# The power -1/2 of the head norms on GpSimd, with table loads, copies of x and the mean in other places

## The reference, cut to what matters

```
def l2norm(t):
    return t / jnp.maximum(jnp.linalg.norm(t, axis=-1, keepdims=True), 1e-12)
...
q = l2norm(q) * qs
k = l2norm(k) * ksc
q = q * cos * scale + rotate_half(q) * sin * scale
k = k * cos * inv + rotate_half(k) * sin * inv
out = local_attention(q, k, v)
...
mu = x.mean(-1, keepdims=True)
var = ((x - mu) ** 2).mean(-1, keepdims=True)
xn = (x - mu) / jnp.sqrt(var + 1e-05) * g + bln
return a * jax.nn.gelu(gate, approximate=False) @ W2 + b2
```

## Time and profile before

| | us |
|---|---|
| median of 3 runs | 3920.88 (3917.01 to 3927.07) |
| the profiled execution | 3918.71 |
| its span | 3916.9 |
| PE busy | 3581.4 (91%) |
| DVE busy | 3162.1 (81%) |
| ACT busy | 2652.5 (68%) |
| POOL busy | 2432.0 (62%) |

### The profile page before, as it was taken

How to read it: one execution, slowest core, us unless ns; L and a number is a source line. 1 busy time by engine, 2 the same in 40 slices (tenths; PEclk the granted TensorE clock), 3 DMA queues, 4 the chain that set the end, 5 groups by cost and what they waited for, 6 DMA issues and landing times.

```text
span 3916.9 us, 146395 instructions
## 1 busy us (share of the span) xinstructions
PE 3581.4 (91%) x60128; PEld 2226.2 (57%) x60128; DVE 3162.1 (81%) x4377; ACT 2652.5 (68%) x4972; POOL 2432.0 (62%) x2197
## 2 busy tenths in 40 slices
PE   5676776899999999999999999999999999999997
PEld 2222222566666666666666666666666666666664
DVE  4899998888878778888878788778787887888884
ACT  3555554677777777767776777677777777676765
POOL 0355554876666666666666666666666666666661
PEclk9889898999999999999999999999999999999999
DMA  3000000111111111111110111111111111110101
GB/s 76 0 0 0 0 0 0 34 32 31 31 42 41 34 30 31 31 47 38 35 32 26 42 42 36 32 31 31 45 37 33 31 31 47 36 36 27 32 28 37
DMA packets 64418, 120.05 MB, mean 31 GB/s; under 512 B 18196, under 2 KB 35986, under 8 KB 63634
## 3 DMA queue, kind: packets, MB, share of 16 engines
q1 hardware_dynamic: 63762, 110.70, 9.7%
HBM read 20.50 MB, written 2.10 MB: 6 GB/s over the span
## 4 chain that ended last, share of the span: by engine, by line
PE 53%; DVE 15%; issue 9%; ACT 7%; POOL 0%; ACTq 0%; DMA 0%; DVEq 0%; POOLq 0%; SPq 0%
PE ob L1187 10%; PE qk L1129 9%; PE sc L1214 7%; PE trb L1001 6%; PE vob L1195 4%; PE vob L1135 4%; PE sc L1163 4%; DVE arena L888 3%; PE sc L1221 3%; DVE ssq L894 3%; DVE mx L901 3%; PE ob L1001 2%; DVE arena L889 2%; ACT arena L619 2%; DVE xnT L978 1%
## 5 line engine op out<-in xcount | busy, mean ns | idle before, releaser
L507 POOL TENSOR_TENSOR arena<-arena,rnorm 128x512 f32<-128x512 f32 x768 | 793.7, 1054 | 929.3 <-ACT rnorm L626 928.8
L500 POOL TENSOR_TENSOR arena<-arena 128x512 f32<-128x512 f32 x768 | 961.7, 1274 | 84.9 <-DVE arena L889 84.9
L633 ACT ACTIVATE arena<-trb 128x512 f32<-128x512 f32 x768 | 465.7, 606 | 432.4 <-PE trb L1001 432.4
L1129 PE MATMUL qk<-wqkv,xs 128*128 128x512 f32 x1536 | 734.2, 601 | 16.0 <-issue 8.9
L888 DVE TENSOR_TENSOR arena<-qk,tab_q 128x512 f32<-128x512 f32 x384 | 263.7, 687 | 504.6 <-ACT arena L619 499.6
L483 POOL TENSOR_TENSOR arena<-arena 128x512 f32<-128x512 f32 x256 | 299.9, 1180 | 345.4 <-DVE arena L858 329.9
L1001 PE MATMUL trb<-ident,arena 128*128 128x128 f32 x3072 | 483.0, 280 | 10.7 <-ACT arena L633 7.6
L619 ACT ACTIVATE arena<-qk 128x512 f32<-128x512 f32 x768 | 433.5, 592 | 79.4 <-PE qk L1129 65.5
L1129 PEld LDWEIGHTS qk<-wqkv,xs 128*128 128x128 f32 x1536 | 294.5, 193 | 312.0 <-issue 294.8
L894 DVE TENSOR_REDUCE ssq<-arena 128x16 f32<-128x1024 f32 x384 | 464.3, 1209 | 0.0
L514 POOL TENSOR_TENSOR arena<-arena,rinv 128x512 f32<-128x512 f32 x384 | 392.4, 1043 | 65.8 <-DVE rinv L911 65.8
(11 more groups left out here) (139 smaller groups left out, 6020.5 us busy)
## 6 DMA issues: line engine op xcount, KB each, us to landing
arena<-arena SPq DMA_DIRECT2D x192, 384.0 KB, 3.2
arena<-arena SPq DMA_DIRECT2D x192, 64.0 KB, 3.0
wqkv<-in_L_ffn_Wqkv SPq DMA_DIRECT2D x18, 512.0 KB, 4.3
wo<-in_L_ffn_Wo SPq DMA_DIRECT2D x6, 512.0 KB, 4.0
arena<-in_L_attn_x SPq DMA_DIRECT2D x8, 256.0 KB, 2.8
out<-arena SPq DMA_DIRECT2D x8, 256.0 KB, 2.2
w<-in_L_ffn_W SPq DMA_DIRECT2D x6, 341.0 KB, 2.9
arena<-in_sel SPq DMA_DIRECT2D x1, 1024.0 KB, 5.0
```

The costliest lines, as they stand in the source:

```text
L500: nc.gpsimd.tensor_tensor(ts[c * 2 + j][:, heads], tu[:, 0, heads], tu[:, 1, heads], ALU.add).then_inc(summed[0], 1)
L507: nc.gpsimd.tensor_tensor(part, part, rnorm[j][:, 8 * h:8 * h + 8].unsqueeze(2).to_broadcast([P, 8, HEAD]), ALU.mult) \
L633: A((qT, kT)[j][u][:, 4 * h:4 * h + 4, at_col:at_col + P], TRB.rearrange("p (a t) -> p a t", a=4), ACT.Copy) \
L1129: MM(QK[:, 512 * h:512 * h + 512], lhsT=xs[u][:, c * P:(c + 1) * P], rhs=wqkv[:, col:col + 512], start=True, stop=True) \
```

## The change

- The clamp of the sums of squares moves from DVE to POOL, and POOL raises them to -1/2 by a two-input instruction with the operation pow and a tile filled with -0.5. ACT's logarithm and exponential for the head norms go. The factors 2^32 (in the logarithm) and 2^16 (in the rotary tables) go too.
- The number of table loads stays at four for a group of eight slots. The loads for gelu stand at the end of slots 6 and 0, those back to the exponential's set in slots 0 and 2 ahead of the exps.
- `stage_x` and `stage_norm` stand in slot 2 ahead of the table load and the exps (`stage_x` of slot 6 ahead of its exps); `stage_norm` was at the end of slot 1.
- PE does the mean of slot 3 behind the two products up.

```diff
-LN_SCALE = float(2 ** 32)
...
+        power = sb("power", [P, HEADS])
...
-        ssqc_ready = sem("ssqc_ready")
-        ln_done = sem("ln_done")
+        ssq_open = sem("ssq_open")
+        ssqc_ready = sem("ssqc_ready", 2)
...
+            nc.gpsimd.memset(power[:], -0.5)
...
             def scale(U, B, u, c, j):
                 item(pool, summed, U * 2 + 1)
+                item(pool, ssq_done, U)
+                pool.sem_inc(ssq_open[0], 1)
+                nc.gpsimd.tensor_scalar(ssqc[j][:], ssq[j][:], NORM_FLOOR, None, ALU.max).then_inc(ssqc_ready[0], 1)
+                item(pool, ssqc_ready, U)
+                nc.gpsimd.tensor_tensor(rnorm[j][:], ssqc[j][:], power[:], ALU.pow).then_inc(r_done[0], 1)
                 pool.wait_ge(r_done[0], U + 1)
...
-            def norms(U, B, u, c, j):
-                act_e.wait_ge(ssqc_ready[0], U + 1)
-                A(lnv[j][:], ssqc[j][:], ACT.Ln, scale=LN_SCALE).then_inc(ln_done[0], 1)
-                act_e.wait_ge(ln_done[0], U + 1)
-                slot(act_e, scaled, U * 2 + 1)
-                A(rnorm[j][:], lnv[j][:], ACT.Exp, scale=-0.5).then_inc(r_done[0], 1)
...
-                if up0 or up1:
-                    act_e.preload_act_table(ACT.Gelu)
...
-                if up0 or up1:
+                if k % UNITS == 2:
+                    at_ = unit_at(l, k, -2)
+                    if at_:
+                        stage_x(at_[1], at_[2], (k + 2) // UNITS % BATCH, l + (k + 2) // LAYER)
+                    at_ = group_at(l, k - 1, LAG_STAGE)
+                    if at_:
+                        stage_norm(*at_)
+                if group_at(l, k - 1, LAG_UP[0]) or group_at(l, k - 1, LAG_UP[1]):
                     act_e.preload_act_table_set(EXP_LN_SET)
                 at_ = step_at(l, k, LAG_SCORES)
                 if at_:
                     exps(*at_)
-                if unit:
-                    norms(*unit)
-                at_ = unit_at(l, k, -2)
-                if at_ and (k + 2) % UNITS == 0:
-                    stage_x(at_[1], at_[2], (k + 2) // UNITS % BATCH, l + (k + 2) // LAYER)
-                at_ = group_at(l, k, LAG_STAGE)
-                if at_:
-                    stage_norm(*at_)
+                if group_at(l, k + 1, LAG_UP[0]) or group_at(l, k + 1, LAG_UP[1]):
+                    act_e.preload_act_table(ACT.Gelu)
...
             def square_sums(U, B, u, c, j):
+                slot(dve, ssqc_ready, U)
                 V.tensor_reduce(ssq[j][:], sq[j].rearrange("p (h e) -> p h e", h=HEADS), op=ALU.add, axis=AX.X).then_inc(ssq_done[0], 1)
-                item(dve, ssq_done, U)
-                V.tensor_scalar(ssqc[j][:], ssq[j][:], NORM_FLOOR, None, ALU.max).then_inc(ssqc_ready[0], 1)
...
-        tab = np.stack([np.cos(freqs) * sc, np.sin(freqs) * sc * sign], 1) * 2.0 ** 16
+        tab = np.stack([np.cos(freqs) * sc, np.sin(freqs) * sc * sign], 1)
```

More of the change, by code:

```diff
@@ L152, in build @@
         ssqc = [sb(f"ssqc{u}", [P, HEADS]) for u in range(2)]
-        lnv = [sb(f"lnv{u}", [P, HEADS]) for u in range(2)]
         rnorm = [sb(f"rnorm{u}", [P, HEADS]) for u in range(2)]
@@ L461, in _ @@
         def _(pool):
-            give_credits(pool, [summed, scaled, hc0_done, hc1_done])
+            give_credits(pool, [summed, scaled, ssqc_ready, hc0_done, hc1_done])
             nc.gpsimd.memset(meanw[:], 1.0 / P)
@@ L1231, in layer_slot @@
                 mean = group_at(l, k, LAG_MEAN)
[L1232 to L1235, removed]
-                    MM(VOB[:, :], lhsT=meanw[:], rhs=xs2.rearrange("p s t -> p (s t)"), start=True, stop=True).then_inc(ln_mean[0], 1)
                 var = group_at(l, k, LAG_VAR)
@@ L1249, in layer_slot @@
                         up(*at_, parts, scored)
+                if mean:
+                    pe.wait_ge(ln_in[0], mean[1] + 1)
+                    if out_before:
+                        item(pe, x_added, out_before[0])
+                    MM(VOB[:, :], lhsT=meanw[:], rhs=xs2.rearrange("p s t -> p (s t)"), start=True, stop=True).then_inc(ln_mean[0], 1)
                 at_ = group_at(l, k, LAG_DOWN)
```

## The result

| | before | after |
|---|---|---|
| median, us | 3922.95 (3917.01 to 3927.07) | 4281.26 (4280.04 to 4284.86) |
| span of the profiled execution | 3916.9 | 4279.6 |
| PE / POOL busy | 3581.4 / 2432.0 | 3702.4 / 3658.3 |

The ratio is 1.0916 (95% interval 1.0897 to 1.0935). The forecast was 3900 with a range to 4200, so it had the wrong sign and its range did not reach the result. What came is the mechanism of its rival 3, POOL as the bound.

The account below looks back on a forecast made before the run. PE was taken to bound the layers, so only its waits could be won. At P = 1.3, -8 (slot 3), -18 (slot 7) and +5 (first slots) made -21 us from 3918.7: 3898, given as 3900, range 3885 to 4200.

Parts of the forecast that it names:

- rival 3: Slower, POOL as the bound of every slot, for P over 2.3; 4090 us at P = 2.7; chance 0.24.
- P: Length of the power on POOL over sixteen columns: between 0.13 and 2.8 us, taken as 1.3.
- x: Time each unit adds to POOL: P + 0.3 us for clamp and handing over, taken as 1.6.
- (a): POOL's other work for two slots is 11.4 of 16.6 us; POOL becomes the bound from P = 2.3.
- (b): First 16 slots, while the pipeline fills: POOL needs 102.9 us against 99.7, so 5 us more with waits.
- (c): Slot 6: the power holds up DVE's L978, which ends 0.28 us after it; beyond P = 1.62 PE waits longer.
- rival 2: Slower, by the power held against L978, P from 1.75 to 2.3: +24 us, 3945 at P = 2.0; chance 0.14.
- slot 7: PE's wait before the products up, 0.42 us a group, nearly all won at P = 1.3: 18 us less.
- Slot 3: PE's wait moves from the mean to the v product; of 1.49 us about 0.17 is kept, 8 us less.
- Rival 4: The whole wait of slot 3 is won because ACT is earlier: -69 us there, 3839 in all; chance 0.04.
- Rival 5: A moved table load delays the next operation by another 1.28 us, in slot 2 before the exps: 3959; chance 0.02.
- The sum: Whole kernel at P = 1.3: -8 for slot 3, -18 for slot 7, +5 for the first slots, -21 us.

Follow-up runs that it names:

- e2: Changed kernel with the power over 8 of the 16 columns, output wrong: 3892.08 us, ratio 0.9919.
- e9: Changed kernel with the power over 12 of the 16 columns, output wrong: 4042.93 us, ratio 1.0306.
- e12: Changed kernel, power kept, POOL's two multiplications that normalise the probabilities cut to one column each, output wrong: 3971.16 us, ratio 1.0119.
- e8: Kernel before with a measurement ahead of it: multiplications and powers of several lengths on POOL, DVE scalings beside some; 3937.8 us in one execution.
- e3: Kernel before with only clamp and power moved to POOL; mean, copies and table loads left in place: 4284.69 us, ratio 1.0922.
- e1: Changed kernel with a multiplication in place of the power on POOL, head norms wrong: 3872.41 us, ratio 0.987.

## Why the prediction was wrong

**The failed step is the size of P.** It took 40 passes, 1.3 us, as "near the middle" between 0.13 and 2.8. The power takes 2.93, just outside the upper bound. In the prediction's unit, a pass of 0.03 us over 16 columns, that is (2.93 - 0.1) / 0.03 = 94 passes; how POOL carries the operation out, in passes or otherwise, no run shows. What they show is 0.158 us for each column. Between ends so far apart, the middle carried no information, yet the forecast got 0.38 on it. The Trainium skill was nearer: by its figure for dependent fp32 chains (GPSIMD Engine Reference, Performance pitfalls for Q7 kernels) and with 40 to 50 steps, a count of its own, the prediction had estimated 2.1 to 2.7 us, and it used this for a rival alone.

**x had a second mis-sized term.** Clamp and handing over were put at 0.30 us and take 0.68: the clamp 0.25 for 0.13, the idle time 0.43 for 0.17. So x is 3.61 where 1.6 was taken, and 2.6 was the point from which POOL becomes the bound. The 0.38 alone is 384 x 0.38 = 146 us of the loss, on the ramp; with P right and 0.3 kept, rival 3's formula would have given 11.4 + 6.46 - 16.6 = 1.26 more for two slots, 32 x 1.26 x 5.6 = 226, and 77.3 + 16 x 3.23 - 99.7 = 29 for the first slots: 255 of the 363 us, or 4176, still inside the stated range. It took the second term to leave it.

**(a) POOL as the bound** was right as a mechanism and close as a threshold. 11.4 us for POOL's other work was 0.3 too much (the two instructions of a pair overlap by some 0.04), and the corner is at P = 1.97 with the real handing over, where 2.3 was forecast. e2, e9 and e12 show flat and ramp; 384 x 0.1 = 38 us for each 0.1 us of P was right (238 for 0.628).

**(b) The first slots.** The direction was right, the amount too small. At P = 1.689 (e2) the first 16 slots take 113.4 us, 13.7 more than before, where the prediction had 5 for 1.3 and 6 for 1.5. And the loss goes on behind them: the first 24 slots lose 20 us in e2 (180.0 for 159.6) and 50 in the changed kernel (210.0).

**(c) The power against L978** was wrong, and rival 2 with it. That L978 is held up by POOL's multiplication was read rightly, and e8 shows the same of a multiplication over 512 columns; the step from there to the power was argued, not shown. e8 refutes it. Besides, VectorE's step never comes behind the power, as the prediction had it: in the changed kernel, e2, e3 and e9 it always starts ahead of the power. In e2 it starts during the clamp 46 times of 48, 0.16 us ahead of the power, and takes 0.49 us, here in that kernel's timeline:

```profile
2155.99 0.74 DVE L971 SCALAR_TENSOR_TENSOR arena<-arena,lpar 128x512 f32<-128x512 f32 x1
...
2156.26 0.57 POOL L506 TENSOR_SCALAR ssqc<-ssq 128x16 f32<-128x16 f32 x1 [1.07 <-DVE ssq L892]
...
2156.76 0.49 DVE L974 TENSOR_SCALAR xnT<-arena,lpar 128x512 f32<-128x512 f32 x1
...
2156.92 1.85 POOL L508 TENSOR_TENSOR rnorm<-ssqc,power 128x8 f32<-128x8 f32 x1
```

By the prediction, P = 1.69 would have won nothing in slot 7; e2 won the 0.43 us of e1. The size offered, 0.42, was right. In the changed kernel itself the gain is not to be seen: L974 meets POOL's addition L500 40 times of 48 and takes 1.37 us.

**Slot 3.** That the wait moves from the mean to the v product was right, link by link; its gain was 0.51 us and not 0.17. Counted from PE's first product, the v product starts 8.20 us later (1714.60 - 1706.40) where 8.64 was worked out. The exps end 0.12 earlier than thought, sums to rope take 1.45 for 1.64, and PE starts 0.06 behind `xc` for 0.15. Of these 0.44 us the slot keeps 0.34, because the v product now starts from rest and takes 0.96 us to the next slot's products, where a streamed one takes 0.86. So 46 x 0.34 = 16 us were missing from the gain. Rival 4 asked for the whole 1.49 and is refuted by e1.

**Table loads.** Rival 5 is refuted: the exps start at 1708.93, 0.01 us behind the load's end (1707.64 + 1.28). The extra drain that the Trainium skill gives (ScalarE: Activation LUTs, What ACT_TABLE_LOAD costs) is not seen here either.

**The sum.** With the power at no length worth naming, the edits give -50 us (e1), where the terms of slots 3 and 7 gave -26. 16 of the difference are slot 3. The layers' last slot, which the prediction did not look at, takes 7.32 us in e1 for 8.9 to 10.1 before, over the five boundaries 8 us more than slot 7's 0.43 each. On the other side stands the power, +409.

## What to carry to other kernels

When work is moved to an engine that is not the bound, add up that engine's work for one period, with what every instruction idles ahead of it, and compare it with the bound's period; the cost is nothing up to the corner and then the full amount, but for stretches in which the bound engine has less to do, such as the first slots here. An operation that no trace shows should not be priced at the middle of wide bounds: time it alone over a few sizes, or say that the forecast rests on a guess. PE's waits were cured here by the place of the mean and of the copies; which of several edits earns the gain is worth separating before one of them is paid for dearly.

## What was unexpected of the hardware

- The power on GpSimd costs 0.40 us and 0.158 us a column of 128 partitions, ten columns as much as 1.9 multiplications over 512 (1.98 against 1.043 us).
- VectorE's scalings of 128 columns run at 0.21 us each beside a 10.55 us power, and beside GpSimd's multiplications of 512 columns only one gets through with each, in 1.27 us or more. The Trainium skill (SBUF — State Buffer, Who interferes with whom) says, for VectorE instructions that take both port pairs, among which it counts `tensor_scalar` from SBUF to SBUF as possible, that whichever instruction starts first holds the shared ports for its whole length. For the multiplication the trace agrees: the scaling that starts at 25.43, behind the multiplication's start at 25.35, ends 0.08 us behind the multiplication's end. For the power it does not.
- The time of a short instruction on GpSimd hardly goes by its columns: a multiplication takes 0.19 us over one column (e8), 0.245 over 16 (e1) and 0.32 over 64 (e8). The clamp is 0.25 us with 0.27 idle ahead of it, though by the view what it waits for, GpSimd's own addition, has just ended; ahead of the power, behind the clamp, it is 0.08. What makes the 0.27 no run shows.
